# Selective-scan kernel: VectorE's product of a unit split in two, and TensorE's order, its folds and the DMA queue rearranged around it

## Chip, cores and metric

The kernel runs on one core of one Trainium2 chip. The metric is device time in microseconds (us) of the whole program, from the first instruction to the last. Engines: TensorE (PE; PEld is its weight load), VectorE (DVE), ScalarE (ACT), GpSimd (POOL), and the sync engine (SP), whose queue issues all DMAs.

## The reference, cut to what matters

Four layers (kinds "cross", "snake", "cross", "causal") on an input of 8 x 64 x 64 x 96. Each layer normalises, projects, convolves, then runs a selective scan in four directions (one in the causal layer), merges the directions and projects back. The part that the change touches is the scan. Per batch, direction, channel d and state n (16 of them):

```
delta = softplus(dts + bias)
dA_t  = exp(delta_t * A)
dBu_t = delta_t * u_t * B_t
h_t   = dA_t * h_(t-1) + dBu_t
y_t   = sum over n of h_t * C_t,  + D * u_t
```

## The kernel before, in words

A layer is an expand stage, a scan stage and a merge stage. The scan stage works through chunks of 1024 positions: 64 chunks in each of the first three layers, 16 in the causal one, 208 in all. A loop body holds two chunks; in a layer with four directions the first runs forward and the second backward. A chunk has three channel tiles (t) of 128 rows; a tile has 16 steps (n), and a step s puts 4 states x 32 channels on the 128 partitions. Two steps are one **unit** v: 8 units to a tile, 24 to a chunk. Units 2, 5 and 7 of a tile are **pool units** (`POOL_UNITS`), the other five I call **vector units**.

For each step VectorE runs one `tensor_tensor_scan` over 1024 positions (`scan`, L1087 for pool units, L1091 for vector units), which needs a decay `exp(delta*A)` and a product `delta*u*B`.

- In a vector unit ScalarE writes the two decays into a ring of three buffers (`decay_of`, L1130). TensorE spreads the unit's B over the partitions into the PSUM tile `slots[:,0,:]` with two bf16 matmuls of 512 columns (`fill_b`, L919). One VectorE product of 2048 columns (`multiply`, L1064) reads that B twice and writes both halves of `slots`, the second half first. The two scans read them.
- In a pool unit GpSimd makes the product (`multiply`, L1312, from B rows that DMAs bring into a ring of two buffers, `load_b`), and ScalarE writes the decays into `slots`, half 0 after the scan that last read it, half 1 likewise.

After both scans GpSimd multiplies the unit's h by C (`gate`, L1291); C rows come by `load_c`. TensorE then sums over the four states: `reduce` (L996) is four fp32 matmuls with 32 output rows each, two units behind the scans (`REDUCE_LAG`), into PSUM `psy`; in unit 5's reduce come two 128-row matmuls for D*u (L990). Each fp32 matmul is two instructions in the profile. The next scan of a ring buffer of h (four of them) waits for its reduce.

Between these, every engine does the coming tile's share, at fixed step numbers. TensorE: `project_delta` at steps 0 and 1 (`DELTA_AT`), `add_up` of four terms at steps 4 to 7 (`SUM_AT`, L956), `project_x` for the next chunk at steps 10 to 14 of tile 0 (`XDBL_AT`, L927). ScalarE: `parts` at step 2 (relu and abs of the projection), `exponential` at 3, `logarithm` at 4, `correction` at 5, `take_delta` at 8, `copy_projected` at (tile 0, steps 12 and 15) (`SAVE_AT`, L1146). A decay for a pool unit is computed at the end of ScalarE's step (`late`), behind that step's share. ScalarE's `copy_y` takes psy to `ybuf` once a tile.

TensorE's order decides when a fill is made. At an even step s it calls `fill_b` for the unit after the one it is at; this waits for the scan that last read slot 0, the first scan of the unit in front. What TensorE does at step s stands behind that wait.

SP's queue follows the gates (`after_gate`): at unit v it waits for the gate of unit v, then issues C for v+4, B for the pool unit after next, du's spreads (8 DMAs each, at units 4 and 7 of a tile) and delta's spreads (8 DMAs each, at units 3 and 4).

Of the kernel before, what the change touches and what calls it, by code (L numbers as in the profile page):

```python
# [61 lines left out]
AHEAD, REDUCE_LAG = 2, 2  # L62
# [9 lines left out]
HI_AT, REST_AT, MID_AT, LESS_MID_AT, LO_AT = (1, 9), (1, 10), (1, 11), (1, 12), (1, 13)  # L72
# [4 lines left out]
DELTA_OUT_AT, DU_OUT_AT = (3, 4), (4, 7)  # L77
LOAD_AT, ROWS_STORE_AT, FLAT_AT, SPLIT_STORE_AT, BC_AT = 2, 6, 8, 13, 15
# [529 lines left out]
def scan_stage(nc, kind, T, W, useq, neg_a, yseq, bcdram, splitdram):  # L608
# [30 lines left out]
    def filled(v):  # L639

        return v + 1 - sum(w <= v for w in on_pool)

# [38 lines left out]
    with ExitStack() as ctx:  # L681
# [33 lines left out]
        slots = ctx.enter_context(nc.psum_tensor("slots" + W["tag"], [P, 2, CH], F32))  # L715
        slot = [slots[:, j, :] for j in range(2)]
# [20 lines left out]
        with nc.Block() as block:  # L737
            @block.sync
            def _(sp):
# [66 lines left out]
                def store_y(i, C0, T_):  # L806
# [6 lines left out]
                    sp.dma_start(yseq[here, t], ybuf[:]).then_inc(sem["y_stored"], 16)  # L813

                def after_gate(i, C0, v):
# [72 lines left out]
                sp.wait_ge(sem["y_stored"], 16 * (NC * TILES + 2))  # L888
# [15 lines left out]
            def _(pe):  # L904
                def fill_b(C0, v, first=False):

                    body, v = v // BU, v % BU
                    q = v // UNITS
                    if v in on_pool:
                        return  # L910
                    S = (C0 + body * BODY_CHUNKS) * STEPS + 2 * v
                    if v % UNITS == 0:
                        pe.wait_ge(sem["bc_in"], (C0 + body * BODY_CHUNKS) * 16 + 16 * (q + 1))
# [3 lines left out]
                    rows_of = batch_of(v) * QUADS + v % QUADS  # L917
                    for cols in HALF:
                        mm = pe.matmul(slot[0][:, cols], pick[:, rows_of, :], bc[q % 2][:, cols],  # L919
# [24 lines left out]
                def add_up(A, term, a):  # L944
# [5 lines left out]
                    if term == 1 and a == 0:  # L950
                        pe.wait_ge(sem["log_ready"], A + 1)
                    if term == 2 and a == 0:
                        pe.wait_ge(sem["excess_ready"], A + 1)
                    if term == 3 and a == 0:
                        pe.wait_ge(sem["exp_ready"], A + 1)
                    mm = pe.matmul(psc[:, HALF[a]], T["ident"][:, :],  # L956
                                   (relu, log, excess, ex)[term][:, HALF[a]], start=(term == 0), stop=(term == 3),
# [20 lines left out]
                def reduce(C0, v):  # L978
# [6 lines left out]
                    if v % TILE_UNITS == SKIP_AT:  # L985
# [3 lines left out]
                        for cols in HALF:  # L989
                            pe.matmul(psy[:, cols], dd[q][:, t, :], u[q][:, t, order][:, cols], start=False, stop=False,  # L990
                                      skip_group_check=True)
                    first = 2 * GROUP * (pair_of(v) % 2)
                    for cols in HALF:
# [25 lines left out]
                fill_b(0, 0, first=True)  # L1019
                with pe.Fori(0, NC // BODY_CHUNKS) as i:  # L1020
                    C0 = i * BODY_CHUNKS
                    for s in range(BS):
                        if s % 2 == 0:
                            fill_b(C0, s // 2 + 1)
                        q, t, n = place(s)
                        after = s // NS + 1
                        if n in DELTA_AT:
# [880 lines left out]
```

## Time and profile before

| | us |
|---|---|
| median of 3 runs | 35480.57 (35474.87 to 35480.98) |
| the profiled execution: its time | 35494.41 |
| the profiled execution: its span | 35492.3 |
| DVE busy | 32715.3 (92%) |
| POOL busy | 30722.6 (87%) |
| PE busy | 25552.7 (72%) |
| ACT busy | 19066.4 (54%) |
| TensorE's granted clock, mean | 0.837 |

Busy shares are means over stages of different kinds. The scan stages are read by themselves, with windows laid from the first scan of each to its last.

### The profile page before, as it was taken

The numbers are of one execution on the slowest core, as the hardware profiler recorded it, in microseconds if no ns is written. First come the engines' busy times: TensorE is split into PE (matmuls) and PEld (weight loads), VectorE is DVE, ScalarE is ACT, GpSimd is POOL, SyncE is SP. The second block draws the span as 40 slices with busy tenths as digits, with TensorE's granted clock in tenths as the row PEclk, the third lists the DMA queues.
The fourth block names the chain that finished last, engine by engine and source line by source line (L and its number), as shares of the span: only waits on it lengthen the run. The fifth ranks groups of instructions, "written<-read, shape, count | busy, mean of one in ns | idle before, by whom it ended". The sixth has DMA issues, their size and how long they took to land. (4 is left out here: it accounts for less than half of the span.)

```text
span 35492.3 us, 317452 instructions
## 1 busy us (share of the span) xinstructions
PE 25552.7 (72%) x72136; PEld 7774.6 (22%) x72136; DVE 32715.3 (92%) x14737; ACT 19066.4 (54%) x23309; POOL 30722.6 (87%) x7768
## 2 busy tenths in 40 slices
PE   6777777777766777777777766777777777766776
PEld 2222222222222222222222222222222222222222
DVE  6999999999976999999999986999999999985995
ACT  5555555555534555555555534555555555544553
POOL 1999999999961999999999961999999999972996
PEclk8888888888888888888888888888888888887888
DMA  5666666666674666666666664666666666675666
GB/s 170 175 176 175 176 176 176 176 176 177 176 217 155 177 177 177 176 177 177 177 177 176 176 208 164 174 176 176 176 176 177 176 177 177 176 207 178 176 177 187
DMA packets 2407103, 6321.11 MB, mean 178 GB/s; under 512 B 701776, under 2 KB 873680, under 8 KB 2395856
## 3 DMA queue, kind: packets, MB, share of 16 engines
q1 hardware_dynamic: 2405328, 6305.89, 67.0%
q14 instruction: 1693, 13.87, 0.1%
q8 instruction: 82, 1.34, 0.0%
HBM read 2904.96 MB, written 764.47 MB: 103 GB/s over the span
## 5 line engine op out<-in xcount | busy, mean ns | idle before, releaser
L1291 POOL TENSOR_TENSOR h<-h,c 128x2048 f32<-128x2048 f32 x4992 | 20766.6, 4180 | 261.9 <-DVE h L1091 165.8
L1091 DVE TENSOR_TENSOR_SCAN h<-decay,state,slots 128x1024 f32<-128x1024 f32 x6240 | 14307.0, 2336 | 126.3 <-ACT state L1235 12.4
L996 PE MATMUL psy<-h,t_fold 128*32 128x512 f32 x40000 | 10436.1, 672 | 4.6 <-POOL h L1291 4.6
L1130 ACT ACTIVATE decay<-delta,na 128x1024 f32<-128x1024 f32 x6248 | 7127.0, 1149 | 2985.8 <-DVE h L1091 2673.9
L1087 DVE TENSOR_TENSOR_SCAN h<-slots,state,made 128x1024 f32<-128x1024 f32 x3744 | 8554.2, 2328 | 132.1 <-ACT slots L1130 131.0
L1312 POOL TENSOR_TENSOR made<-du,b 128x2048 f32<-128x2048 f32 x1872 | 7821.6, 4178 | 676.8 <-DMA b<-bcdram 676.8
L919 PE MATMUL slots<-bc,pick 96*128 96x512 bf16 x6248 | 2328.0, 461 | 7926.1 <-DVE h L1087 6871.9
L1064 DVE TENSOR_TENSOR slots<-du,slots 128x2048 f32<-128x2048 f32 x3120 | 7165.4, 2297 | 700.8 <-PE slots L919 298.6
L1130 ACT ACTIVATE slots<-delta,na 128x1024 f32<-128x1024 f32 x3744 | 4173.5, 1116 | 4990.3 <-DVE h L1091 4988.7
L996 PEld LDWEIGHTS psy<-h,t_fold 128*32 128x32 f32 x40000 | 2201.8, 120 | 7758.5 <-issue 7507.4
L1304 POOL TENSOR_TENSOR du<-delta,u 128x1024 f32<-128x1024 f32 x628 | 1477.0, 2352 | 2260.1 <-ACT delta L1184 2260.1
L919 PEld LDWEIGHTS slots<-bc,pick 96*128 96x128 bf16 x6248 | 371.3, 101 | 10723.2 <-DVE h L1087 8571.5
L1138 ACT COPY state<-h 128x2 f32<-128x2 f32 x4992 | 931.8, 187 | 2308.5 <-DVE h L1091 1353.7
L956 PE MATMUL psc<-relu,t_ident 128*128 128x512 f32 x2512 | 1922.6, 911 | 9.2 <-ACT ex L1154 9.2
L927 PE MATMUL psc<-u,wx 128*96 128x512 f32 x2544 | 1654.5, 788 | 237.0 <-DMA bdt<-in_bdt 236.4
L990 PE MATMUL psy<-u,dd 128*128 128x512 f32 x2496 | 1753.0, 843 | 0.0
L1184 ACT COPY delta<-psc 128x1024 f32<-128x1024 f32 x628 | 637.8, 1016 | 1552.0 <-PE psc L956 1552.0
L956 PE MATMUL psc<-log,t_ident 128*128 128x512 f32 x2512 | 1411.9, 691 | 55.4 <-ACT log L1167 55.4
L937 PE MATMUL psc<-dts,wdt 32*128 32x512 f32 x2512 | 1436.6, 696 | 0.9 <-ACT dts L1218 0.9
L956 PE MATMUL psc<-excess,t_ident 128*128 128x512 f32 x2512 | 1181.9, 592 | 0.0
L956 PE MATMUL psc<-ex,t_ident 128*128 128x512 f32 x2512 | 1180.4, 592 | 0.0
L1747 POOL TENSOR_TENSOR tn<-tn,zc 128x1536 f32<-128x1536 f32 x96 | 347.0, 3615 | 959.5 <-ACT tn L1615 922.7
(119 smaller groups left out, 19140.2 us busy)
## 6 DMA issues: line engine op xcount, KB each, us to landing
delta<-delta SPq DMA_DIRECT2D x10048, 128.0 KB, 2.6
du<-du SPq DMA_DIRECT2D x10048, 128.0 KB, 3.0
b<-bcdram SPq DMA_DIRECT2D x7520, 128.0 KB, 2.8
c<-bcdram SPq DMA_DIRECT2D x6720, 128.0 KB, 2.9
u<-useq SPq DMA_DIRECT2D x212, 1536.0 KB, 6.9
yseq<-ybuf SPq DMA_DIRECT2D x624, 512.0 KB, 2.9
useq<-ready SPq DMA_DIRECT2D x84, 2048.0 KB, 6.6
ya<-yseq SPq DMA_DIRECT2D x288, 512.0 KB, 4.9
```

What stands on the lines that cost most here:

```text
L919: mm = pe.matmul(slot[0][:, cols], pick[:, rows_of, :], bc[q % 2][:, cols], start=True, stop=True)
L927: mm = pe.matmul(psc[0:96, HALF[a]], wx[q][:, s, :], u[q][:, s, HALF[a]], start=(s == 0), stop=(s == TILES - 1))
L956: mm = pe.matmul(psc[:, HALF[a]], T["ident"][:, :], (relu, log, excess, ex)[term][:, HALF[a]], start=(term == 0), stop=(term == 3), skip_g ...
L990: pe.matmul(psy[:, cols], dd[q][:, t, :], u[q][:, t, order][:, cols], start=False, stop=False, skip_group_check=True)
L996: mm = pe.matmul(psy[rows, cols], T["fold"][:, :], h[v % H_RING][:, c, cols], start=(v % QUADS == 0), stop=(v % QUADS == QUADS - 1), skip_ ...
L1064: dve.tensor_tensor(slots[:, ::-1, :], du4[j % DU_RING][:, ::-1, 1:], slots[:, 0:1, :].broadcast_to((P, 2, CH)), ALU.mult)\
L1087: dve.tensor_tensor_scan(out, slot[s % 2][:, order], made[p % MADE_RING][:, s % 2, order], first, ALU.mult, ALU.add).then_inc(sem["h_ready ...
L1091: dve.tensor_tensor_scan(out, decay[s % DECAY_RING][:, order], slot[s % 2][:, order], first, ALU.mult, ALU.add).then_inc(sem["h_ready"], 1)
L1130: act.activation(dst, delta4[j % DELTA_RING][:, s % 2, :], ACT.Exp, scale=na[q][:, k:k + 1])\
L1291: pool.tensor_tensor(both[:, :, 0:CH], both[:, :, 1:], c4[g][:, order].unsqueeze(1).broadcast_to((P, 2, CH)), ALU.mult)\
L1304: pool.tensor_tensor(du[:], delta[:, 1:], u[q][:, t, :], ALU.mult).then_inc(sem["du_ready"], 1)
L1312: pool.tensor_tensor(made[k % MADE_RING][:], du4[j % DU_RING][:, :, 1:], b4[k % B_RING][:].unsqueeze(1).broadcast_to((P, 2, CH)), ALU.mult)\
```

## The change

Five edits go together.

1. **Products and fills per step.** `multiply` becomes two products of 1024 columns, one per step, each in its own PSUM tile (`slot0`, `slot1`). TensorE fills both (`fill_b` per step, so twice the matmuls). The wait of the product for the scans in front is gone; what keeps it right is that the fill waits for the scan that last read the slot.
2. **TensorE's order.** At an odd step s it makes the fills for s+1 and s+2 (`FILL_LAG` = 2); the second waits for the scan of s itself. Its other work moves to odd steps, behind those fills: both halves of `project_delta` at step 1, the terms of `add_up` at 3, 3, 5, 5, 5, 5, 7, 7 in the order relu, exp, log, excess, and `project_x` three matmuls at step 11 and three at 13.
3. **Folds.** The four matmuls of `reduce` go to four different column groups of TensorE (32 output rows each), where they went to two; the D*u matmuls become four with 64 output rows.
4. **psy's new layout** asks for a rearranged `copy_y` (same size) and two stores of half the size for each y.
5. **The queue.** At a gate, B goes in front of C; delta's second half moves from unit 4 to unit 6; the stores and loads of the split rows move by two or three units.

```diff
-DELTA_AT = (0, 1)
+DELTA_AT = (1, 1)
-SUM_AT = (4, 4, 5, 5, 6, 6, 7, 7)
+SUM_AT = (3, 3, 5, 5, 5, 5, 7, 7)
-XDBL_AT = [(0, 10), (0, 10), (0, 11), (0, 12), (0, 13), (0, 14)]
-SAVE_AT = [(0, 12), (0, 15)]
+XDBL_AT = [(0, 11), (0, 11), (0, 11), (0, 13), (0, 13), (0, 13)]
+SAVE_AT = [(0, 12), (0, 14)]
-DELTA_OUT_AT, DU_OUT_AT = (3, 4), (4, 7)
+DELTA_OUT_AT, DU_OUT_AT = (3, 6), (4, 7)
...
+                    if new_b:
+                        load_b(on_pool.index(v) + B_RING)
                     if new_c:
                         load_c(v + QUADS)
-                    if new_b:
-                        load_b(on_pool.index(v) + B_RING)
...
-                        mm = pe.matmul(slot[0][:, cols], pick[:, rows_of, :], bc[q % 2][:, cols],
+                        mm = pe.matmul(slot[s % 2][:, cols], pick[:, rows_of, :], bc[q % 2][:, cols],
...
-                    first = 2 * GROUP * (pair_of(v) % 2)
-                    for cols in HALF:
+                    bank = HALF[pair_of(v) % 2]
+                    for a, cols in enumerate(HALF):
                         for c in range(2):
-                            rows = slice(first + GROUP * c, first + GROUP * c + GROUP)
-                            mm = pe.matmul(psy[rows, cols], T["fold"][:, :], h[v % H_RING][:, c, cols],
+                            rows = slice(2 * GROUP * a + GROUP * c, 2 * GROUP * a + GROUP * c + GROUP)
+                            mm = pe.matmul(psy[rows, bank], T["fold"][:, :], h[v % H_RING][:, c, cols],
...
                     for s in range(BS):
-                        if s % 2 == 0:
-                            fill_b(C0, s // 2 + 1)
+                        if s % 2 == 1:
+                            fill_b(C0, s - 1 + FILL_LAG)
+                            fill_b(C0, s + FILL_LAG)
...
-                    dve.wait_ge(sem["h_ready"], C0 * STEPS + (2 * v + H_START))
-                    dve.tensor_tensor(slots[:, ::-1, :], du4[j % DU_RING][:, ::-1, 1:],
-                                      slots[:, 0:1, :].broadcast_to((P, 2, CH)), ALU.mult)\
-                        .then_inc(sem["b_multiplied"], 2)
+                    dve.tensor_tensor(slot[s % 2][:], du4[j % DU_RING][:, s % 2, 1:], slot[s % 2][:], ALU.mult)\
+                        .then_inc(sem["b_multiplied"], 1)
```

## Rows read from the trace of the kernel before

**Rows 1.** Windows: us, then busy us of PE, PEld, DVE, ACT, POOL.

```profile
11483.00:20870.00 9387.00, 6922.73 (x19830) 2031.56 (x19831) 9190.60 (x4032) 5310.99 (x6598) 9163.81 (x2302) 0.84 0.69 176
...
sum 30579.00, PE 22509.03 PEld 6621.48 DVE 29871.26 ACT 17258.57 POOL 29779.13; mean PE 5627.26 PEld 1655.37 DVE 7467.82 ACT 4314.64 POOL 7444.78
```

**Rows 2.** Timeline of DVE: start us, us, operation; x2 merges two.

```profile
2005.45 2.30 DVE L1064 TENSOR_TENSOR slots<-du,slots 128x2048 f32<-128x2048 f32 x1
2007.78 4.59 DVE L1091 TENSOR_TENSOR_SCAN h<-decay,state,slots 128x1024 f32<-128x1024 f32 x2
2012.28 4.57 DVE L1087 TENSOR_TENSOR_SCAN h<-slots,state,made 128x1024 f32<-128x1024 f32 x2
2016.96 2.30 DVE L1064 TENSOR_TENSOR slots<-du,slots 128x2048 f32<-128x2048 f32 x1
```

**Rows 3.** Timeline of POOL in the same stage.

```profile
2089.83 12.45 POOL L1291 TENSOR_TENSOR h<-h,c 128x2048 f32<-128x2048 f32 x3
2102.22 4.17 POOL L1312 TENSOR_TENSOR made<-du,b 128x2048 f32<-128x2048 f32 x1
...
2127.02 2.33 POOL L1304 TENSOR_TENSOR du<-delta,u 128x1024 f32<-128x1024 f32 x1
2129.31 4.17 POOL L1291 TENSOR_TENSOR h<-h,c 128x2048 f32<-128x2048 f32 x1
```

**Rows 4.** Waits, whole span: us in total, times, longest us.

```profile
POOL made L1312 <- DMA b<-bcdram: 676.8, 208, 31.1
...
DVE slots L1064 <- PE slots L919: 298.6, 129, 64.5
...
DVE h L1087 <- ACT slots L1130: 131.0, 130, 3.7
```

**Rows 5.** Timeline of DVE in the first expand stage.

```profile
207.44 1.27 DVE L557 SCALAR_TENSOR_TENSOR acc<-xp,convw,ps_t 128x1024 f32<-128x1024 f32 x1
208.63 4.47 DVE L573 SCALAR_TENSOR_TENSOR acc<-xp,convw,acc 128x4096 f32<-128x4096 f32 x1
```

**Rows 6.** Timeline of PE, from a fill to the fill after next's share.

```profile
2014.67 1.04 PE L919 MATMUL slots<-bc,pick 96*128 96x512 bf16 x2 [2.08 <-DVE h L1087]
...
2022.16 0.60 PE L919 MATMUL slots<-bc,pick 96*128 96x512 bf16 x2
```

**Rows 7.** The same, one tile later.

```profile
2063.30 1.03 PE L919 MATMUL slots<-bc,pick 96*128 96x512 bf16 x2 [5.42 <-DVE h L1087]
2064.13 3.62 PE L956 MATMUL psc<-relu,t_ident 128*128 128x512 f32 x4
...
2070.22 1.91 PE L996 MATMUL psy<-h,t_fold 128*32 128x512 f32 x8
2072.06 0.61 PE L919 MATMUL slots<-bc,pick 96*128 96x512 bf16 x2
```

**Rows 8.** Timeline of DVE: the product behind that last fill.

```profile
2072.89 2.29 DVE L1064 TENSOR_TENSOR slots<-du,slots 128x2048 f32<-128x2048 f32 x1 [0.39 <-PE slots L919]
```

**Rows 9.** Windows; the number behind POOL's is the granted clock of TensorE.

```profile
2042.00:2045.00 3.00, 0.31 (x1) 0.13 (x2) 3.00 (x3) 2.58 (x4) 3.00 (x2) 0.50 0.93 214
...
2063.00:2069.00 6.00, 5.70 (x8) 2.49 (x9) 5.86 (x4) 6.00 (x8) 6.00 (x2) 0.50 0.47 144
2070.00:2079.00 9.00, 9.00 (x33) 2.87 (x34) 8.58 (x5) 3.48 (x4) 9.00 (x3) 1.00 0.70 234
```

**Rows 10.** Timeline of PE: the next chunk's projection at steps 10 and 11.

```profile
2082.55 4.44 PE L927 MATMUL psc<-u,wx 128*96 128x512 f32 x6
```

**Rows 11.** Timeline of ACT behind it.

```profile
2087.10 0.58 ACT L1146 COPY rows<-psc 64x512 f32<-64x512 f32 x1 [2.58 <-PE psc L927]
2087.70 0.58 ACT L1147 COPY dts<-psc 32x512 f32<-32x512 f32 x1
2089.11 1.12 ACT L1130 ACTIVATE slots<-delta,na 128x1024 f32<-128x1024 f32 x1 [0.83 <-DVE h L1091]
```

**Rows 12.** Timeline of SP's queue at the end of a chunk.

```profile
2189.04 5.22 SPq L796 DMA_DIRECT2D delta<-delta  x8
...
2196.46 1.84 SPq L781 DMA_DIRECT2D b<-bcdram  x4
```

More of the change, by code:

```diff
@@ L637, in place @@
         return s // STEPS, s // NS % TILES, s % NS
-    def filled(v):
-        return v + 1 - sum(w <= v for w in on_pool)
     def by_vector(s):
@@ L714, in scan_stage @@
         state = sb("state", [P, 2, TILES * NS])
-        slots = ctx.enter_context(nc.psum_tensor("slots" + W["tag"], [P, 2, CH], F32))
-        slot = [slots[:, j, :] for j in range(2)]
+        slot = [ctx.enter_context(nc.psum_tensor(f"slot{j}" + W["tag"], [P, CH], F32)) for j in range(2)]
         psc = ctx.enter_context(nc.psum_tensor("psc" + W["tag"], [P, CH], F32))
@@ L812, in store_y @@
                         here = here + SEQS[kind] * PAIRS * NCH
-                    sp.dma_start(yseq[here, t], ybuf[:]).then_inc(sem["y_stored"], 16)
+                    halves = yseq[here, t].rearrange("(r p) (a f) -> a p r f", r=2, a=HALVES)
+                    for a in range(HALVES):
+                        sp.dma_start(halves[HALVES - 1 - a if backward(q) else a],
+                                     ybuf[2 * GROUP * a:2 * GROUP * a + 2 * GROUP, :].rearrange("p (r f) -> p r f", r=2))\
+                            .then_inc(sem["y_stored"], 16)
                 def after_gate(i, C0, v):
@@ L904, in _, with fill_b @@
             def _(pe):
[L905 to L909, printed above, removed]
+                def fill_b(C0, s, first=False):
+                    body, s = s // BS, s % BS
+                    q, t, n = place(s)
+                    if s // 2 in on_pool:
                         return
-                    S = (C0 + body * BODY_CHUNKS) * STEPS + 2 * v
-                    if v % UNITS == 0:
+                    S = (C0 + body * BODY_CHUNKS) * STEPS + s
+                    if t == 0 and n == 0:
                         pe.wait_ge(sem["bc_in"], (C0 + body * BODY_CHUNKS) * 16 + 16 * (q + 1))
@@ L950, in add_up @@
                     if term == 1 and a == 0:
+                        pe.wait_ge(sem["exp_ready"], A + 1)
+                    if term == 2 and a == 0:
                         pe.wait_ge(sem["log_ready"], A + 1)
-                    if term == 2 and a == 0:
+                    if term == 3 and a == 0:
                         pe.wait_ge(sem["excess_ready"], A + 1)
-                    if term == 3 and a == 0:
-                        pe.wait_ge(sem["exp_ready"], A + 1)
                     mm = pe.matmul(psc[:, HALF[a]], T["ident"][:, :],
-                                   (relu, log, excess, ex)[term][:, HALF[a]], start=(term == 0), stop=(term == 3),
+                                   (relu, ex, log, excess)[term][:, HALF[a]], start=(term == 0), stop=(term == 3),
                                    skip_group_check=True)
@@ L988, in reduce @@
                         order = slice(None, None, -1) if backward(q) else slice(None)
-                        for cols in HALF:
-                            pe.matmul(psy[:, cols], dd[q][:, t, :], u[q][:, t, order][:, cols], start=False, stop=False,
-                                      skip_group_check=True)
-                    first = 2 * GROUP * (pair_of(v) % 2)
-                    for cols in HALF:
+                        for r in range(2):
+                            chans = slice(2 * GROUP * r, 2 * GROUP * r + 2 * GROUP)
+                            for a, cols in enumerate(HALF):
+                                pe.matmul(psy[2 * GROUP * a:2 * GROUP * a + 2 * GROUP, HALF[r]], dd[q][:, t, chans],
+                                          u[q][:, t, order][:, cols], start=False, stop=False, skip_group_check=True)
+                    bank = HALF[pair_of(v) % 2]
+                    for a, cols in enumerate(HALF):
                         for c in range(2):
-                            rows = slice(first + GROUP * c, first + GROUP * c + GROUP)
-                            mm = pe.matmul(psy[rows, cols], T["fold"][:, :], h[v % H_RING][:, c, cols],
+                            rows = slice(2 * GROUP * a + GROUP * c, 2 * GROUP * a + GROUP * c + GROUP)
+                            mm = pe.matmul(psy[rows, bank], T["fold"][:, :], h[v % H_RING][:, c, cols],
                                            start=(v % QUADS == 0), stop=(v % QUADS == QUADS - 1),
@@ L1018, in _ @@
                 pe.wait_ge(sem["pick_in"], 16)
-                fill_b(0, 0, first=True)
+                for s in range(FILL_LAG):
+                    fill_b(0, s, first=True)
                 with pe.Fori(0, NC // BODY_CHUNKS) as i:
```

48 lines of the change are left out of this document (26 added, 22 removed).

## The prediction

> **What bounds the kernel now.** I read the page first: VectorE and GpSimd are both nearly full, so a mean over the span says little, and I laid windows on the four scan stages. They take 30,579 us together [rows 1]; over 208 chunks that is 147.0 us a chunk. The profiled execution took 35,494 us, so 4,915 us lie outside and stay.
>
> Then the timeline of VectorE, from start to start. A product is followed by its scans after 2.33 us. Two scans of a vector unit in front of a pool unit take 4.50 us; two scans in front of a product take 4.68 [rows 2], because the product waits for them to end, where scans follow each other 0.09 us before the end of the one in front (4.59 long, 4.50 apart). A tile has five vector units (two followed by a vector unit, three by a pool unit) and three pool units, each followed by a vector unit: 5 x 2.33 + 2 x 4.68 + 3 x 4.50 + 3 x 4.68 = 48.55 us, 145.7 us a chunk. VectorE stands still for only 1.3 of the 147.0.
>
> GpSimd is close behind. Three gates take 12.39 us (4.13 each), delta times u 2.29 [rows 3]: 11 x 4.13 + 2.29 = 47.7 us a tile, 143.2 us a chunk. It waits 208 times for B, 676.8 us [rows 4]: once a chunk, 3.25 us. So VectorE sets the pace, GpSimd could follow at 143.2, and no change can gain more than 3.8 us a chunk, 790 us in all, unless GpSimd's own work shrinks.
>
> TensorE isn't full, but its clock matters. After a stretch in which it did next to nothing (0.31 of 3 us) its granted clock is 0.50, 1.2 GHz, and it stays there through the first 6 us of dense work; later it is 1.00, 2.4 GHz [rows 9]. A fill is two matmuls, 0.60 us at the high clock and 1.04 at the low one [rows 6]. From its start to the start of the product that waited for it there are 0.83 us at the high clock [rows 7, 8]; at the low clock I add the difference, 1.26.
>
> **VectorE's own work.** The product of 2048 columns takes 2.30 us; half of it is 1.15. The trace has no product of 1024 columns with a PSUM operand in these stages. The nearest operation starts 1.19 us before the next one and lasts 1.27 [rows 5]. A fixed part that doesn't overlap would give 1.24. I take 1.15, since scans here start 0.09 us before the end of the one in front and 1.24 less 0.09 is 1.15; the bounds are 1.15 and 1.24. The wait of the product for the scans goes, so 4.68 becomes 4.50. A vector unit is then 2 x 1.15 + 4.50 = 6.80 us, a pool unit 4.50, a tile 5 x 6.80 + 3 x 4.50 = 47.5, a chunk **142.5 us: 3.2 us less** than 145.7 (2.0 less at 1.19, 0.5 less at 1.24).
>
> A rule speaks against this. The Trainium skill (VectorE: DVE Perf Modes, The DRAIN you can't avoid) says that the next VectorE operation doesn't start until the one in front has emptied the pipe, and that one should minimise the number of operations. The trace doesn't agree where no wait stands between: the scans start 0.09 us early [rows 2]. By the rule a chunk would be 15 x (2 x 1.24 + 2 x 2.34) + 9 x 4.68 = 149.5 us before any stall.
>
> Now what the new order asks of TensorE. E is the end of the last scan of a unit. I count what comes late, by place; all of it is added to 142.5, for VectorE no longer has anything to wait out.
>
> **The fill of slot 1.** It can start only when the second scan of the unit in front has read the slot: a fill starts 0.06 us after the end of its scan (2012.28 and one scan of 2.33, then 2014.67) [rows 2, 6]. The first product starts at E - 0.09, the second could start at E + 1.06. At the high clock B is there at E + 0.89: nothing lost. At the low clock at E + 1.32: 0.26 us lost. Before, the one fill had a whole scan as its cover. I take the low clock at about half of the five vector units of a tile, those behind an idle stretch of TensorE: units 0, 3 and 6 mostly, 1 sometimes, 4 never (it follows dense work). 0.26 x 2.4 x 3 = **1.9 us a chunk**; the bounds are 0 and 3.9.
>
> **The four terms at step 5.** `add_up` has four matmuls at one step, then a reduce, and only then come the fills of unit 4. Before, the same amount stood between two fills: fill, four matmuls, reduce, next fill took 7.49 us in one tile and 8.76 in the next [rows 6, 7]. There the start was the pool unit's first scan, now it is its second, 2.25 us later, and the fill is due 6.80 - 0.09 - 0.83 = 5.9 us after E. The folds get shorter: eight instructions in 1.84 us now, two column groups at a time (four full-width instructions at the low clock take 3.62, so half of that at the high one) [rows 7]; four groups would be 0.92. That gives 6.6 and 7.8 us for these tiles, and 4.8 where the clock is high all along (0.45 + 3.4 + 0.95). Late by nothing, 0.8, or 1.7 (less 0.26 where the second product was late too). With three in ten tiles at the high clock, four in the middle and three low: 0.75 a tile, **2.2 us a chunk**; bounds 0 and 5. What is queued behind: the fill, so VectorE's product, so everything.
>
> The Trainium skill (TensorE: Matmul & The Clock Gate, Part 3) has three column tiles of 32 columns at 2.38 times the rate of one. By a rate of that size, an estimate from the page, four folds would take about 3.4 / 2.4 = 1.4 us and the term would be 0.5 us a tile higher; the trace shows full overlap for two groups and nothing for four.
>
> **The projection at steps 11 and 13.** `project_x` now starts behind the fill that waits for the second scan of unit 5. Its three matmuls and the way to ScalarE's copy took 4.55 us (2082.55 to 2087.10) [rows 10, 11], 5.3 if the clock is low throughout (1.7 a matmul [rows 7]). Copies can start at E + 0.06 + 0.83 + 4.55 to 5.3, that is 5.4 to 6.2; two copies are 1.2 us, and behind them on ScalarE stands the decay of pool unit 7, 1.12 us [rows 11]: E + 7.9 to 8.7 with the overlap and signal. Its scan is due at E - 0.09 + 6.80 = 6.7. Late 1.2 to 2.0 us, once a chunk; at the high clock (3 x 0.85) nothing. Before, the projection started a scan earlier, and scans of pool units already waited 131.0 us in 130 places for such decays [rows 4]. I take **1.4 us a chunk**; bounds 0.3 and 2.0.
>
> **delta's projection at step 1.** Both halves now stand behind the fill for step 3, which waits for E of unit 0. At the high clock they are done at E + 2.4, relu and abs (1.1 each, a ScalarE pass of 1024 columns [rows 11]) at E + 4.6, just when the first decay of unit 2 may be written anyway. At the low clock all is 2.1 us later: the first decay 1.1 us late, the second, with two more passes in front of it, 0.95 more. The dense work in front (D*u, folds, fill) mostly lifts the clock here; at one tile in eight: **0.7 us a chunk**; bounds 0 and 3.
>
> **The queue.** At the end of a chunk delta's second half (5.22 us of issues) stands in front of B [rows 12]: that is the wait of 3.25 us on GpSimd. Moved to unit 6, and B in front of C, B is issued some 7 us earlier and the wait goes. It costs and gains nothing by itself while VectorE sets the pace; it takes away GpSimd's lag, and with it some of VectorE's 1.3 us. delta's second half is used only half a tile later, C four units later: both keep their cover. Three more issues a chunk for y are nothing. I keep 0.5 us of the 1.3.
>
> **The sum.** 142.5 + 1.9 + 2.2 + 1.4 + 0.7 + 0.5 = 149.2 us a chunk, against 147.0. Times 208: 31,034; with 4,915: 35,949 us in a profiled execution, and the median of the runs stands 14 us below its own: **35,940 us, 1.3% slower**.
>
> **Rivals.**
> - *GpSimd's pace.* TensorE's clock keeps up, fills and terms land in time, and VectorE at 142.5 runs into GpSimd at 143.2. With about 1 us for the ends of stages, 144.3 a chunk: 34,920 us. For it: less TensorE time in folds, fills that land 0.17 us early at the high clock. Against: shorter folds leave TensorE more idle stretches, and behind those it is slow [rows 9]. It decides once slot 1's fill takes under 1.0 us and the work of step 5 under 5.9.
> - *Half as late.* The stalls are there but sum to 3.3 instead of 6.7 (145.8): 35,230 us. Each of my terms hangs on how often the clock is low.
> - *Later still.* Four folds don't overlap better than two (0.9 us more at step 5, 2.7 a chunk): 151.9, 36,500 us. By the skill's rule on draining, 149.5 + 6.7 = 156.2, 37,390 us.
> - *Nothing.* GpSimd without its waits and VectorE with new ones balance at 147: 35,480 us.
>
> **Chances and range.** Forecast 0.46 (35,600 to 36,300 as its own range); GpSimd's pace 0.16; half as late 0.24, of which 0.04 ends within 0.2%; nothing 0.04; later still 0.10, of it 0.02 for the drain. About 0.2%, 70 us, is what a measurement of this kernel can tell from no change. Faster 0.36, the same 0.08, slower 0.56. Half of the GpSimd case below 35,000 and the tail above 36,400 are left out: 35,000 to 36,400.
>
> **What would show it.** Products 1.24 us long and 1.15 apart; VectorE's waits for fills rising from 298.6 us to over 800, the longest ones at unit 4; waits for decays over 131 us, at unit 7 of tile 0; GpSimd's wait for B gone and in its place waits for VectorE's h; folds of eight instructions in some 0.95 us; the mean clock below 0.84. I am wrong if TensorE's clock holds up, if products don't overlap, or if GpSimd is never idle.

## The result, and the profile after

The changed kernel takes 35,216.1 us (median of 4 executions, 35,184.3 to 35,233.9) against 35,480.8: ratio 0.9923, 95% interval 0.9907 to 0.9939. Beside other kernels in a later group it took 35,182.1 against 35,472.5 (0.9919, 0.9902 to 0.9935). So the change is worth some 265 to 290 us, 0.8%. I had forecast 35,940, 1.3% slower. What came true is the rival "half as late" (35,230 us).

The windows on the scan stages, as in [rows 1], the second stage and the sum of all four:

```profile
11383.00:20688.00 9305.00, 6449.02 (x22512) 1679.73 (x22512) 9111.41 (x4991) 5268.83 (x6598) 9160.78 (x2302) 0.79 0.71 178
...
sum 30296.00, PE 20946.60 PEld 5465.74 DVE 29617.67 ACT 17123.81 POOL 29767.77; mean PE 5236.65 PEld 1366.43 DVE 7404.42 ACT 4280.95 POOL 7441.94
```

30,296 / 208 = 145.6 us a chunk, from 147.0: 283 us in all, so the whole gain lies in the scan stages (the two profiled executions are 273 us apart). TensorE is busy for 1,560 us less there and its mean granted clock falls from 0.84 to 0.79.

The timeline of VectorE, for the spacing of [rows 2]; `x2` merges two operations:

```profile
14018.19 2.34 DVE L1071 TENSOR_TENSOR slot<-du,slot 128x1024 f32<-128x1024 f32 x2
14020.44 4.58 DVE L1097 TENSOR_TENSOR_SCAN h<-decay,state,slot 128x1024 f32<-128x1024 f32 x2
...
14032.41 4.57 DVE L1093 TENSOR_TENSOR_SCAN h<-slot,state,made 128x1024 f32<-128x1024 f32 x2
14036.90 2.44 DVE L1071 TENSOR_TENSOR slot<-du,slot 128x1024 f32<-128x1024 f32 x2
14039.25 4.58 DVE L1097 TENSOR_TENSOR_SCAN h<-decay,state,slot 128x1024 f32<-128x1024 f32 x2
14045.77 4.59 DVE L1093 TENSOR_TENSOR_SCAN h<-slot,state,made 128x1024 f32<-128x1024 f32 x2 [1.94 <-ACT slot L1137]
...
14065.34 2.35 DVE L1093 TENSOR_TENSOR_SCAN h<-slot,state,made 128x1024 f32<-128x1024 f32 x1 [1.40 <-ACT slot L1137]
14068.16 2.35 DVE L1093 TENSOR_TENSOR_SCAN h<-slot,state,made 128x1024 f32<-128x1024 f32 x1 [0.47 <-ACT slot L1137]
```

From the start of two products to the start of their scans there are 2.25 us (14018.19 to 14020.44), and a pair of scans in front of a product takes 4.49 (14032.41 to 14036.90), as much as in front of another scan. In the pair at 14036.90 the merged length is 2.44 instead of 2.34: there the second product waited 0.10 us for slot 1's fill. The fill on TensorE, and that second product by itself:

```profile
14037.04 1.03 PE L920 MATMUL slot<-bc,pick 96*128 96x512 bf16 x2 [1.21 <-DVE h L1093]
```

```profile
14038.11 1.23 DVE L1071 TENSOR_TENSOR slot<-du,slot 128x1024 f32<-128x1024 f32 x1
```

The product starts 1.07 us after the start of this fill, which runs at the low clock (two matmuls in 1.03 us).

The large stalls are behind decays: 1.94 us at step 14 of tile 0, then 1.40 and 0.47 at steps 4 and 5 of the next tile.

The waits of the whole span, as in [rows 4] (us in total, times, longest):

```profile
DVE h L1093 <- ACT slot L1137: 564.8, 594, 2.9
POOL h L1299 <- DVE h L1093: 358.4, 222, 2.4
DVE slot L1071 <- PE slot L920: 286.1, 78, 64.6
```

GpSimd's 208 waits for B are gone (123.6 us are left, in four places at the starts of stages), and in their place it waits for VectorE's h. Waits for fills did not rise (298.6 before), though this view leaves out the 0.10 us of the second products; waits for decays rose from 131.0 to 564.8.

For the stalls by place I took every start-to-start spacing of VectorE's products and scans in the second scan stage (64 chunks) and subtracted the shortest usual spacing of its kind (after: 1.115 product to product, 1.127 product to scan, 2.24 to 2.26 behind a scan; before: 2.33 product to scan, 2.41 to 2.43 from a scan to a product that waits for it). The sum of these spacings is VectorE's own work. In us a chunk:

| | before | forecast | after |
|---|---|---|---|
| VectorE's own work | 145.5 | 142.5 | 141.4 |
| slot 1's fill late (second product) | none | 1.9 | 0.5 |
| fills of unit 4 late (the terms at step 5) | 0.2 | 2.2 | 0.1 |
| decays late at step 14 of tile 0 (projection) | 0.4 | 1.4 | 1.3 |
| decays late at steps 4 and 5 (delta's projection) | none | 0.7 | 1.6 |
| the rest, mostly at the start of a chunk | 0.6 | 0.5 | 0.5 |
| chunk | 146.7 | 149.2 | 145.4 |

### The profile page after: what moved, and what is told of

It reads as the page before. It is cut to its first block and busy times, and to the rows that moved or that the text cites. A ratio compares the mean times of both kernels' runs of the same rounds, so it can differ in the third digit from the quotient of the medians.

```text
span 35219.2 us, 342636 instructions
## 1 busy us (share of the span) xinstructions
PE 23995.8 (68%) x80880; PEld 6621.3 (19%) x80880; DVE 32458.7 (92%) x17857; ACT 18928.9 (54%) x23309; POOL 30713.0 (87%) x7768
## 5 line engine op out<-in xcount | busy, mean ns | idle before, releaser
L1097 DVE TENSOR_TENSOR_SCAN h<-decay,state,slot 128x1024 f32<-128x1024 f32 x6240 | 14285.7, 2332 | 25.4 <-ACT state L1243 25.4
L920 PE MATMUL slot<-bc,pick 96*128 96x512 bf16 x12496 | 4722.5, 468 | 8878.4 <-DVE h L1093 7278.9
L1093 DVE TENSOR_TENSOR_SCAN h<-slot,state,made 128x1024 f32<-128x1024 f32 x3744 | 8584.3, 2330 | 573.1 <-ACT slot L1137 564.8
L1320 POOL TENSOR_TENSOR made<-du,b 128x2048 f32<-128x2048 f32 x1872 | 7822.8, 4179 | 123.6 <-DMA b<-bcdram 123.6
L1071 DVE TENSOR_TENSOR slot<-du,slot 128x1024 f32<-128x1024 f32 x6240 | 7400.0, 1215 | 330.5 <-PE slot L920 286.1
L1000 PE MATMUL psy<-h,t_fold 128*32 128x512 f32 x40000 | 6105.1, 704 | 0.0
L1137 ACT ACTIVATE slot<-delta,na 128x1024 f32<-128x1024 f32 x3744 | 4157.4, 1113 | 3213.4 <-DVE h L1097 3213.1
L920 PEld LDWEIGHTS slot<-bc,pick 96*128 96x128 bf16 x12496 | 752.4, 102 | 13883.2 <-DVE h L1093 10547.2
L993 PE MATMUL psy<-u,dd 128*64 128x512 f32 x4992 | 1969.5, 933 | 0.0
L1000 PEld LDWEIGHTS psy<-h,t_fold 128*32 128x32 f32 x40000 | 953.8, 119 | 4572.6 <-issue 3911.2
L1160 ACT ACTIVATE relu<-psc,bdt 128x1024 f32<-128x1024 f32 x628 | 699.2, 1113 | 1872.1 <-PE psc L938 1872.1
```

The lines of the kernel that those rows point to most:

```text
L920: mm = pe.matmul(slot[s % 2][:, cols], pick[:, rows_of, :], bc[q % 2][:, cols], start=True, stop=True)
L993: pe.matmul(psy[2 * GROUP * a:2 * GROUP * a + 2 * GROUP, HALF[r]], dd[q][:, t, chans], u[q][:, t, order][:, cols], start=False, stop=False ...
L1000: mm = pe.matmul(psy[rows, bank], T["fold"][:, :], h[v % H_RING][:, c, cols], start=(v % QUADS == 0), stop=(v % QUADS == QUADS - 1), skip_ ...
L1071: dve.tensor_tensor(slot[s % 2][:], du4[j % DU_RING][:, s % 2, 1:], slot[s % 2][:], ALU.mult)\
L1093: dve.tensor_tensor_scan(out, slot[s % 2][:, order], made[p % MADE_RING][:, s % 2, order], first, ALU.mult, ALU.add).then_inc(sem["h_ready ...
L1097: dve.tensor_tensor_scan(out, decay[s % DECAY_RING][:, order], slot[s % 2][:, order], first, ALU.mult, ALU.add).then_inc(sem["h_ready"], 1)
```

## The experiments

Every kernel here computes everything. "Chunk" and "stall" are worked out as in the table above, from the second scan stage.

### The queue by itself

`queue_alone` is the kernel before with edit 5's order of loads.

```diff
-DELTA_OUT_AT, DU_OUT_AT = (3, 4), (4, 7)
+DELTA_OUT_AT, DU_OUT_AT = (3, 6), (4, 7)
...
+                    if new_b:
+                        load_b(on_pool.index(v) + B_RING)
                     if new_c:
                         load_c(v + QUADS)
-                    if new_b:
-                        load_b(on_pool.index(v) + B_RING)
```

> The kernel before with the queue's part of the change alone: B in front of C at a gate, delta's second half at unit 6. Theory: VectorE set the pace before, and GpSimd's wait for B (3.25 us once a chunk) was hidden; what can go is VectorE's own wait at the first product of a chunk, 0.3 of 147.0 us. Time 35,400 to 35,480. Rival: GpSimd with its wait (143.2 + 3.25 = 146.4 us a chunk) was as much the bound, and the queue brought the gain of 265 us: about 35,220.

Measured: 35,334.3 us against 35,474.6, ratio 0.9959 (0.9946 to 0.9973): 140 us faster, between the two theories and outside mine. GpSimd's waits, in its own trace:

```profile
POOL h L1291 <- DVE h L1091: 435.4, 628, 9.1
POOL h L1291 <- DVE h L1087: 198.4, 626, 1.3
POOL made L1312 <- DMA b<-bcdram: 123.4, 4, 31.0
```

GpSimd waits 553 us less for B and 376 us more for VectorE (634 against 258 before). VectorE's stall falls from 1.17 to 0.77 us a chunk. The four stages together are 162 us shorter, and most of it is in one place, the decay at step 14 of tile 0: it was late by 1.14, 0.36 and 0.66 us a chunk in the first three stages, together 138 us, and is late by 0.05 or less now. So GpSimd's lag had reached VectorE there; by which operations, I did not follow.

`queue_undone` is the changed kernel with the old order (the same lines the other way round).

> The changed kernel with the old queue: C in front of B, delta's second half at unit 4. Theory: beside VectorE's new 145.6 us a chunk, GpSimd with the wait for B stands at 143.2 + 3.25 = 146.4 and becomes the bound: 146.5 to 147 us a chunk, 35,390 to 35,480, with some 600 to 700 us of waits for B on GpSimd. Rival: GpSimd's wait still hides behind VectorE: 35,216 as the changed kernel.

Measured: 35,436.2 us, ratio 0.9988 (0.9979 to 0.9998), as expected. So beside the other edits the queue is worth 220 us (250 against the repeat of the changed kernel). The wait for B is back, waits for decays are 628.2 us, and the stall at step 14 grows from 1.3 to 2.1 us a chunk.

```profile
POOL made L1320 <- DMA b<-bcdram: 642.4, 209, 30.8
```

### The folds

`folds_undone` is the changed kernel with edits 3 and 4 taken back.

```diff
-                    bank = HALF[pair_of(v) % 2]
-                    for a, cols in enumerate(HALF):
+                    first = 2 * GROUP * (pair_of(v) % 2)
+                    for cols in HALF:
                         for c in range(2):
-                            rows = slice(2 * GROUP * a + GROUP * c, 2 * GROUP * a + GROUP * c + GROUP)
-                            mm = pe.matmul(psy[rows, bank], T["fold"][:, :], h[v % H_RING][:, c, cols],
+                            rows = slice(first + GROUP * c, first + GROUP * c + GROUP)
+                            mm = pe.matmul(psy[rows, cols], T["fold"][:, :], h[v % H_RING][:, c, cols],
```

> The changed kernel with the old folds (two column groups), the old layout of psy, one store for each y. Theory: folds are off the path; a reduce takes 1.85 us instead of 1.0, TensorE is fuller and its mean clock higher than 0.79, and the fill behind step 5 is late by at most 0.3 us a tile: 35,200 to 35,430. Rival: shorter folds are what made room for the second fill; without them 35,480 or more.

Measured: 35,143.6 us, ratio 0.9905 (0.9890 to 0.9920), a little faster than the change (0.9923 and 0.9919) and faster than I expected. The intervals overlap and the groups differ, so I say only that the folds bring nothing. TensorE's groups by line, first of the change, then of this kernel (busy us, mean ns of one instruction):

```profile
L1000 PE MATMUL psy<-h,t_fold 128*32 128x512 f32 x40000 | 6105.1, 704 | 0.0
L957 PE MATMUL psc<-relu,t_ident 128*128 128x512 f32 x2512 | 2047.0, 964 | 617.4 <-ACT ex L1161 617.4
...
L938 PE MATMUL psc<-dts,wdt 32*128 32x512 f32 x2512 | 1564.0, 750 | 4.9 <-issue 4.0 <-ACT dts L1226 0.9
L957 PE MATMUL psc<-ex,t_ident 128*128 128x512 f32 x2512 | 1263.7, 627 | 0.0
L957 PE MATMUL psc<-log,t_ident 128*128 128x512 f32 x2512 | 1191.8, 597 | 0.0
```

```profile
L993 PE MATMUL psy<-h,t_fold 128*32 128x512 f32 x40000 | 10195.6, 677 | 0.0
...
L953 PE MATMUL psc<-relu,t_ident 128*128 128x512 f32 x2512 | 1308.5, 644 | 140.4 <-ACT ex L1154 140.4
L934 PE MATMUL psc<-dts,wdt 32*128 32x512 f32 x2512 | 1291.8, 634 | 0.9 <-ACT dts L1218 0.9
```

The folds save 4,090 us of TensorE, and in return two operations on the way to the decays are slower: delta's projection 750 ns instead of 634, the relu terms 964 instead of 644. The exp terms are not (627 against 664), nor the log terms. Mean clock 0.788 against 0.855. With the old folds VectorE's stall at steps 4 and 5 is 0.1 us a chunk instead of 1.6, but longer folds make fills late in tile 2 instead (0.8 at step 8, 0.5 at step 2). The sums are equal: 4.1 and 4.0.

`core_alone` takes back the queue and the folds and keeps edits 1 and 2.

> The changed kernel with the old queue and the old folds: what is left is the products per step, B in both slots and TensorE's order. Theory: GpSimd with its wait for B (143.2 + 3.25 = 146.4 us a chunk) holds it, so most of the gain is lost without the queue: 35,370 to 35,450. Rival: the gains add, 330 us for all less 140 for the queue: 35,285.

Measured: 35,373.5 us, ratio 0.9967 (0.9955 to 0.9979), 109 us faster, at the edge of what I expected. Its stall is 5.0 us a chunk, of it 2.1 at step 14.

In this table 5 stands for the order of loads alone; the rows without it keep the new places of the split rows.

| edits in | against before |
|---|---|
| 5 | -140 us |
| 1 and 2 | -109 us |
| 1, 2 and 3, 4 | -38 us |
| 1, 2 and 5 | -331 us |
| all | -265 and -290 us |

Edits 1 and 2 and the queue together give 331 us, more than their 249 one by one. With the folds the number is smaller in both pairs (by 71 us without the queue, 40 to 65 with it), but in each pair the intervals touch or overlap, so a cost of the folds is likely and not shown.

### The product

`split_alone` is the kernel before with its product cut in two, both still reading the one B, and the waits left as they were.

```diff
-                    dve.tensor_tensor(slots[:, ::-1, :], du4[j % DU_RING][:, ::-1, 1:],
-                                      slots[:, 0:1, :].broadcast_to((P, 2, CH)), ALU.mult)\
-                        .then_inc(sem["b_multiplied"], 2)
+                    for a in (1, 0):
+                        dve.tensor_tensor(slot[a], du4[j % DU_RING][:, a, 1:], slot[0], ALU.mult)\
+                            .then_inc(sem["b_multiplied"], 1)
```

> The kernel before with its product of 2048 columns made as two of 1024, still from one slot of B, still behind the wait for the scans, and the scans behind both. Theory: the split itself gains nothing; 1.115 + 1.24 us take the place of 2.33, so +0.03 us in 3120 units, about +90 us: 35,480 to 35,590. What the change gains on VectorE (145.5 to 141.4 us a chunk of operations) is the waits that B in both slots takes away. Rival: two short products are faster than one long by themselves: under 35,400.

Measured: 35,453.8 us, ratio 0.9993 (0.9984 to 1.0002): no difference, a little under what I expected.

```profile
14013.92 2.36 DVE L1065 TENSOR_TENSOR slots<-du,slots 128x1024 f32<-128x1024 f32 x2
14016.32 4.58 DVE L1091 TENSOR_TENSOR_SCAN h<-decay,state,slots 128x1024 f32<-128x1024 f32 x2
14020.82 4.57 DVE L1087 TENSOR_TENSOR_SCAN h<-slots,state,made 128x1024 f32<-128x1024 f32 x2
14025.42 2.36 DVE L1065 TENSOR_TENSOR slots<-du,slots 128x1024 f32<-128x1024 f32 x2
```

Two products cost nothing over one, and by themselves gain nothing: 2.40 us to the scans (14013.92 to 14016.32) where one product had 2.33, and 4.60 for the scans in front of them (14020.82 to 14025.42) where there were 4.68. The gain of edit 1 is in the waits of VectorE for itself. Without them the changed kernel has 2.25 and 4.49. In single spacings, from a scan to a product that waits for it there were 2.41 to 2.43 us between starts, now 2.24; from the single product to its scan 2.33, now 1.115 + 1.127 = 2.24. Five times (0.18 + 0.09) a tile, three tiles: 4.1 us a chunk.

### The four terms

`terms_at_5_and_7` makes step 5 what I had feared: relu comes there too, as TensorE's first work behind an idle stretch.

```diff
-SUM_AT = (3, 3, 5, 5, 5, 5, 7, 7)
+SUM_AT = (5, 5, 5, 5, 7, 7, 7, 7)
```

> The changed kernel with add_up's terms at steps 5, 5, 5, 5, 7, 7, 7, 7: still four matmuls at step 5, but none at step 3. Theory: my error at step 5 was TensorE's clock, which the relu terms and the fold at step 3 lift or keep up; without them TensorE has done little since step 1, the four matmuls run at 1.2 GHz as in the kernel before, and the fill of unit 4 is 1 to 1.7 us late in most tiles: 148.5 to 150 us a chunk, 35,800 to 36,100. Rival: the place of the terms is harmless (the shorter folds alone made the burst fit): 35,216, within 0.2%.

Measured: 35,888.1 us, ratio 1.0116 (1.0101 to 1.0132), as the theory said. Timelines of TensorE and of VectorE in this kernel, and one window on TensorE's burst (the number behind POOL's is the granted clock):

```profile
14024.46 1.03 PE L920 MATMUL slot<-bc,pick 96*128 96x512 bf16 x2 [1.79 <-DVE h L1093]
14025.28 3.62 PE L957 MATMUL psc<-relu,t_ident 128*128 128x512 f32 x4
14028.70 2.80 PE L957 MATMUL psc<-ex,t_ident 128*128 128x512 f32 x4
...
14032.43 1.04 PE L920 MATMUL slot<-bc,pick 96*128 96x512 bf16 x4
```

```profile
14033.07 2.36 DVE L1071 TENSOR_TENSOR slot<-du,slot 128x1024 f32<-128x1024 f32 x2 [1.83 <-PE slot L920]
```

```profile
14025.00:14028.00 3.00, 3.00 (x6) 1.36 (x5) 3.00 (x3) 3.00 (x5) 3.00 (x1) 0.50 0.80 208
```

Here four terms and a fold stand between fills from 14025.28 to 14032.43, 7.15 us, and the product comes 1.8 us late. That is the case that I priced at 0.75 us a tile; it costs 0.8 here (2.4 us a chunk at step 8). Of the 3.5 us a chunk that this kernel is longer than the changed one, 2.3 is this; decays at step 4 of tile 1 and slot 1's fills take most of the rest. The same place in the changed kernel:

```profile
14064.20 3.31 PE L957 MATMUL psc<-relu,t_ident 128*128 128x512 f32 x4 [0.43 <-ACT ex L1161]
...
14071.01 1.88 PE L957 MATMUL psc<-ex,t_ident 128*128 128x512 f32 x4
14072.73 1.88 PE L957 MATMUL psc<-log,t_ident 128*128 128x512 f32 x4
14074.54 1.06 PE L1000 MATMUL psy<-h,t_fold 128*32 128x512 f32 x8
14075.54 0.61 PE L920 MATMUL slot<-bc,pick 96*128 96x512 bf16 x2
```

```profile
14064.00:14067.00 3.00, 2.80 (x4) 1.17 (x4) 1.66 (x1) 2.97 (x4) 2.98 (x1) 0.51 0.93 247
14071.00:14077.00 6.00, 5.15 (x19) 1.60 (x17) 6.00 (x4) 4.42 (x6) 6.00 (x2) 1.00 0.80 221
```

The relu terms run at step 3, at the low clock (0.51), where nothing is due behind them; two steps later the clock is high (1.00) and four terms and a fold are done in 4.5 us.

### The late decays

Two places stall VectorE behind decays. ScalarE's timeline in the changed kernel, at step 14 of tile 0, then at steps 4 and 5 of tile 1:

```profile
14043.30 0.58 ACT L1153 COPY rows<-psc 64x512 f32<-64x512 f32 x1 [6.09 <-PE psc L928]
...
14044.38 2.15 ACT L1137 ACTIVATE slot<-delta,na 128x1024 f32<-128x1024 f32 x2
...
14061.93 1.11 ACT L1160 ACTIVATE relu<-psc,bdt 128x1024 f32<-128x1024 f32 x1 [4.61 <-PE psc L938]
...
14063.94 1.12 ACT L1137 ACTIVATE slot<-delta,na 128x1024 f32<-128x1024 f32 x1
...
14067.03 1.10 ACT L1137 ACTIVATE slot<-delta,na 128x1024 f32<-128x1024 f32 x1
```

and TensorE's work in front of them:

```profile
14037.86 5.32 PE L928 MATMUL psc<-u,wx 128*96 128x512 f32 x6
...
14058.12 3.78 PE L938 MATMUL psc<-dts,wdt 32*128 32x512 f32 x4
```

Both matmul groups ran at the low clock (granted 0.50 from 14037 to 14042 and from 14058 to 14062), and in both places the decay stands behind the operation that waited for them. `save_later` moves only the copies of the projection, `delta_earlier` only delta's projection, `both_moved` both.

```diff
-SAVE_AT = [(0, 12), (0, 14)]
+SAVE_AT = [(0, 13), (0, 15)]
```

> The changed kernel with copy_projected at steps 13 and 15 of tile 0 instead of 12 and 14, so that ScalarE makes the first decay of unit 7 before it waits for the projection. Theory: VectorE's wait of 1.27 us a chunk at step 14 of tile 0 goes, VectorE sets the pace: 144.3 to 144.6 us a chunk, 34,930 to 35,010. Rival: the wait is hidden in GpSimd's lag or comes back at the next step: 35,150 to 35,220.

Measured: 35,054.8 us, ratio 0.9877 (0.9862 to 0.9893). The stall at step 14 falls from 1.3 to 0.2 us a chunk, as wanted; a part of it comes back at step 8 (0.1 to 0.7), which I had not expected, and the time is 45 us above my range.

```diff
-DELTA_AT = (1, 1)
+DELTA_AT = (0, 0)
```

> The changed kernel with both halves of project_delta at step 0, ahead of the two fills of step 1. Theory: relu and abs then come before the first decay of unit 2 is due; the waits at steps 4 and 5 (1.42 us a chunk in tile 1, 0.22 in tile 0) go: 144.0 to 144.3 us a chunk, 34,870 to 34,950. Rival: the projection's matmuls in front of the fill for step 2 make that fill late instead: 35,200 or more.

> Both of these moves. Theory: VectorE alone would need 145.6 - 2.9 = 142.7 us a chunk, under GpSimd's 143.2, so GpSimd sets the pace: 143.6 to 144.2 us a chunk, 34,790 to 34,910, GpSimd nearly without waits in the scan stages, and less than the sum of the two gains. Rival: GpSimd isn't a bound and the gains add: 34,600 to 34,650.

Measured: 36,193.9 us, ratio 1.0200 (1.0185 to 1.0216), and 36,134.9, 1.0185 (1.0169 to 1.0200). Both theories fell, the first by over 1,200 us. The decays at steps 4 and 5 did come in time, as wanted. But TensorE, in `delta_earlier`, now had its work too early:

```profile
14041.94 1.04 PE L920 MATMUL slot<-bc,pick 96*128 96x512 bf16 x4
...
14044.31 1.96 PE L957 MATMUL psc<-relu,t_ident 128*128 128x512 f32 x4 [0.34 <-ACT ex L1161]
...
14051.73 0.61 PE L920 MATMUL slot<-bc,pick 96*128 96x512 bf16 x2 [4.47 <-DVE h L1093]
...
14054.80 3.62 PE L957 MATMUL psc<-ex,t_ident 128*128 128x512 f32 x4
14058.21 2.34 PE L957 MATMUL psc<-log,t_ident 128*128 128x512 f32 x4
```

The relu terms run at the high clock, TensorE idles for 4.47 us, and the four terms of step 5, in front of which it now has only two fills, take the low clock: 5.75 us (14054.80 to 14058.21 + 2.34) for what took 3.6 above (14071.01 to 14072.73 + 1.88). Fills of unit 4 are late by 3.6 us a chunk: this is `terms_at_5_and_7` by another road. Those of unit 1 are late by 3.2, and that is another cause, the rival of my expectation: the fills at 14041.94 stand behind delta's projection, and the product that needs them waits 1.01 us here.

`decay_first` tries ScalarE's side: both decays of unit 2 go in front of `parts` and `exponential`. `decay_first_save_later` adds the move of the copies, `decay_first_save_later_old_folds` takes back the folds as well.

```diff
+                            first = late and n in (PARTS_AT, EXP_AT)
+                            if first:
+                                decay_of(i, s + AHEAD)
                             if n == PARTS_AT:
...
-                            if late:
+                            if late and not first:
                                 decay_of(i, s + AHEAD)
```

> The changed kernel with ScalarE's decays for unit 2 made ahead of parts (step 2) and of exponential (step 3), which then come 2 to 3 us later; TensorE's order is untouched. Theory: the waits at steps 4 and 5 (1.64 us a chunk) go, and because the relu terms now run later and not earlier, TensorE still comes to step 5 at the high clock: 144.0 to 144.4 us a chunk, 34,880 to 34,970. Rival: log and excess come too late for TensorE's burst at step 5, and the fill of unit 4 is late instead: 35,150 or more.

> The same with copy_projected at steps 13 and 15 as well. Theory: VectorE alone could do 143.0 or less, GpSimd's own work is 143.2, so GpSimd sets the pace with 0.5 to 1 us of waits: 143.7 to 144.3 us a chunk, 34,810 to 34,930. Rival: the gains add without regard to GpSimd: under 34,780.

> That version with the old folds in two column groups. Theory: with the decays out of the way the old folds only fill TensorE: its fill behind step 5 is late by 0.3 to 0.5 us in some tiles, but GpSimd sets the pace: the same as the version with four groups within 0.2%. Rival: the old folds are better by themselves, as in the changed kernel: 0.2% or more under it.

Measured: 36,504.2 us, ratio 1.0291 (1.0274 to 1.0308); 36,176.2, 1.0198 (1.0181 to 1.0215); 36,831.4, 1.0383 (1.0366 to 1.0400). All three theories fell. TensorE and VectorE in `decay_first`:

```profile
14056.25 3.63 PE L957 MATMUL psc<-relu,t_ident 128*128 128x512 f32 x4 [4.27 <-ACT ex L1161]
...
14060.81 1.04 PE L920 MATMUL slot<-bc,pick 96*128 96x512 bf16 x4
```

```profile
14061.45 2.36 DVE L1071 TENSOR_TENSOR slot<-du,slot 128x1024 f32<-128x1024 f32 x2 [1.82 <-PE slot L920]
```

The decay waits for a scan before it can be written; `parts` now stands behind it, the relu terms on TensorE stand behind `parts`, and the fills of unit 3 stand behind those: 2.4 to 3.1 us late in every tile.

So only what no one waits for may go behind a decay. `exp_later_save_later` leaves `parts` where it is, moves the second decay alone in front of `exponential` (`first = late and n == EXP_AT`), and has the later copies.

> The changed kernel with copy_projected at steps 13 and 15, and only the second decay of unit 2 made ahead of exponential (step 3); parts stays ahead of the first decay, so the relu terms come as early as in the changed kernel. Theory: the wait at step 5 (0.6 us a chunk) goes beside that at step 14, nothing gets later at step 6: 0.4 to 0.7 us a chunk under save_later alone: 34,900 to 34,980. Rival: exp comes 1 to 2 us later, and TensorE's burst at step 5 waits for it or for log: 35,050 or more.

Measured: 34,935.4 us (34,927.6 to 34,960.5) against 35,482.2, ratio 0.9847 (0.9832 to 0.9862), as expected and the fastest of all: 547 us under before, some 250 to 280 under the change.

Waits for decays are down to 181.0 us, from 564.8. VectorE stands for 2.9 us of a chunk of 144.2, of which 0.9 at step 4 of tile 1. GpSimd needs 143.2, so little more is to be had here.

`save_later_old_folds` asks whether the folds can now go back.

> The changed kernel with the old folds and copy_projected at steps 13 and 15. Theory: the old folds keep TensorE fuller and its clock up, so there is no wait for decays at steps 4 and 5, and with the wait at step 14 (1.6 us a chunk) gone the chunk is 144.0 to 144.5: 34,830 to 34,950. Rival: the fills behind step 7 and the D*u matmuls, already 1.3 us a chunk late, take it back: 35,050 or more.

Measured: 35,202.5 us, ratio 0.9922 (0.9907 to 0.9937). The theory fell and the rival was right. Its fills are late in tile 2 and at the first unit of tile 1, and step 14 still stalls by 0.9 us a chunk. With the later copies the shorter folds are worth 148 us (35,054.8 against 35,202.5); without them they were worth nothing. `change_again` is the repeat of the changed kernel given with the result.

> The changed kernel once more, beside the others of this group, because the version with the old folds came out 0.2% under it in another group. Theory: the difference is real and this one stays at 35,190 to 35,240. Rival: it was a difference between chips or groups: 35,140 to 35,160 here.

Measured: 35,182.1 us, ratio 0.9919 (0.9902 to 0.9935), between the theory and the rival. So a part of the 0.2% by which `folds_undone` lay under the change goes with the repeat, and the rest stays within the intervals.

## Why the prediction was wrong

- *What bounds the kernel.* Right: VectorE sets the pace, GpSimd can follow at 143.2, and the best version found stops at 144.2.
- *VectorE's own work.* Right in kind, too small in size: 4.1 us a chunk gained where I had 3.2. Products last 1.215 us and start 1.115 apart, not 1.15, and scans start 2.24 to 2.26 us apart. The rule that I set against it from the Trainium skill (VectorE: DVE Perf Modes, The DRAIN you can't avoid) would have had each product start only after the one in front; products here start 0.10 us before the end of the one in front. I had left out the exception that the same paragraph makes for an operation that isn't held, with which the trace agrees.
- *The fill of slot 1.* Mis-sized: 1.9 forecast, 0.5 measured. The second product waits where the clock is low, as said, but for 0.10 us and not 0.26, and in 5.2 of the 15 vector units of a chunk, not 7.2. From the low-clock fill to its product there are 1.07 us (14037.04 to 14038.11); I had 1.26. Adding the difference of two fill durations (1.04 and 0.60) was right: without the old wait a product starts 0.64 us after the start of a high-clock fill (14032.43 to 14033.07 in `terms_at_5_and_7`), and 1.07 is 0.43 more. What was wrong was the 0.83 that I added it to. I read it from a product that also waits for VectorE's own scans, a wait that edit 1 takes away.
- *The four terms at step 5.* **This step failed, and together with slot 1's fill it decides the sign**: 2.2 forecast, 0.1 measured. The mechanism is real: `terms_at_5_and_7` shows it at nearly my price. What I had wrong was the clock at that place. I took the mix of clocks at step 5 from [rows 7], where the relu terms are the first work after an idle stretch, though the change moves those very terms to step 3. They now take the low clock there (964 ns), and the exp terms and log terms behind them run at 627 and 597, where 592 is what the excess terms take in both kernels. I costed the move of the terms and did not move the clock with them. A slip beside it, which nearly cancels: a fill due 5.9 us after E and made at 6.6 or 7.8 is late by 0.7 or 1.9, not 0.8 or 1.7.
- *The projection at steps 11 and 13.* Right: 1.4 forecast, 1.3 measured, in the place named, and `save_later` takes it away.
- *delta's projection at step 1.* The chain is right, its frequency is not: I gave it one tile in eight, and in tile 1 it happens in nearly every chunk (1.6 us over all tiles instead of 0.7, of it 1.4 in tile 1). `folds_undone` gives the reason: at that place the shorter folds leave the clock low.
- *The folds.* Eight instructions in 1.00 us (14074.54 to 14075.54), I had 0.92, against 1.84 before (2070.22 to 2072.06 in [rows 7]). So four groups overlap nearly fully here. The Trainium skill (TensorE: Matmul & The Clock Gate, Part 3) gives 2.38 times the rate of one for three column tiles; carried over to four it had given my estimate of 1.4 us, which the trace doesn't bear out. The saving helps step 5 less than I had it: with the old folds the fills of unit 4 are late by 0.8 us a chunk, in tile 2 alone.
- *The queue.* My sentence that it gains nothing while VectorE sets the pace is wrong: 140 us alone. Yet the sum had it under VectorE's idle time (0.5 kept of 1.3, 0.8 us a chunk or 166 us), which is near the 162 us measured in the scan stages. The place, step 14, I had not named.
- *The signs to look for.* Mean clock below 0.84, B's wait gone, waits for decays up at unit 7 of tile 0: seen. Waits for fills over 800 us: not seen (286). Folds of 0.95 us: 1.00. Products 1.24 us long and 1.15 apart: 1.215 and 1.115.

Of the difference of 3.8 us a chunk, 2.1 is the four terms, 1.4 slot 1's fill and 1.1 VectorE's own work, and delta's projection takes 0.9 back; the last 0.1 is step 14.

What stays open: why the queue is worth more beside edits 1 and 2 than alone. Without it the decays at step 14 are 0.8 us a chunk later, the same place where the queue alone gains, but I did not follow GpSimd's lag to them operation by operation.

## What to carry to other kernels

When a change moves work on an engine whose granted clock is low behind idle stretches, as TensorE's is here, move the clock with it: ask for each deadline what runs in front of it after the change, not what ran there before. In this kernel a short low-clock job two steps ahead of a dense burst, where nothing waits for it, pays for the burst (4.5 us instead of 7.15); work done too early leaves an idle stretch and makes the burst slow (5.75 us for the terms that took 3.6). And before an operation is put in front of another on an in-order engine, follow what stands behind the one that is held: two decays brought forward cost 1,320 us because an operation that another engine waits for stood behind them.

## What the hardware showed that I had not expected

- Saving 4,090 us of TensorE time with the fold in four column groups gained nothing in the changed kernel, and lowered the mean clock from 0.855 to 0.788.
- Doing delta's projection one step earlier cost 2.8% over the change (36,193.9 against 35,216.1 us), part of it through the clock at step 5, part because fills stand behind the projection.
- With operations of 1024 columns, a VectorE product that waits for the scan in front starts 0.11 us later than one that doesn't (4.60 us for the two scans in front of it in `split_alone`, 4.49 in the changed kernel). A product of 2048 columns is no cheaper than two of 1024: from its scan in front to its own scan, 4.68 + 2.33 us, against 4.60 + 2.40.
- In the changed kernel a product starts 1.07 us after the start of a low-clock fill that it waited for and 0.64 us after that of a high-clock one. In the kernel before it is 0.83 at the high clock ([rows 7, 8]), where the product waits for VectorE's scans as well; in `split_alone`, with that wait and products of 1024 columns, it is 0.80. So most of the 0.19 seems to go with the wait, though the scans that it is for had ended by then (0.39 us before, in [rows 8]).
